# A float32 attend over four column quadrants, with scores and exponentials one head further ahead, and a part of a gate product in the last heads

## What is computed

```python
attn = _attention(rmsnorm(x, ln1_w), Wq, Wk, Wv, Wo)   # 16 heads of 32, causal, 512 x 512 probabilities
mod = 0.1 * tanh(attn @ A)                             # A: 512 x 16
h = rmsnorm(x, ln2_w)
gate = silu(h @ W_in.T + mod * (h @ A) @ B)            # 2048 wide
up = h @ W_up.T
out = x + gate * up @ W_down.T
```

## Time and profile before

| | |
|---|---|
| median of 3 runs | 1033.87 us |
| profiled execution | 1034.01 us |
| span from its first to its last instruction | 1032.3 us |
| TensorE busy | 1006.2 us (97%) |
| VectorE busy | 703.2 us (68%) |
| ScalarE busy | 604.1 us (59%) |
| GpSimd busy | 279.5 us (27%) |
| granted TensorE clock, mean | 0.998 |

### The profile page before, as it was taken

How to read it: one execution, slowest core, us unless ns; L and a number is a source line. 1 busy time by engine, 2 the same in 40 slices (tenths; PEclk the granted TensorE clock), 3 DMA queues, 4 the chain that set the end, 5 groups by cost and what they waited for, 6 DMA issues and landing times.

```text
span 1032.3 us, 16767 instructions
## 1 busy us (share of the span) xinstructions
PE 1006.2 (97%) x5140; PEld 831.6 (81%) x5141; DVE 703.2 (68%) x1841; ACT 604.1 (59%) x1447; POOL 279.5 (27%) x276
## 2 busy tenths in 40 slices
PE   6999999999999999999999999999999999999998
PEld 6787888877888888778888888778888887888886
DVE  7766756996665559985664489966655599754443
ACT  4464456996434448985344379963444499843332
POOL 4537124861000117640000148600001187300000
PEclk9999999999999999999999999999999999999999
DMA  6545124344232426434232354343334254222321
GB/s 233 194 161 173 41 100 117 82 93 163 92 91 91 132 60 183 95 111 147 91 92 91 113 159 93 77 166 96 94 100 145 58 157 101 84 82 91 91 91 52
DMA packets 47073, 115.78 MB, mean 112 GB/s; under 512 B 6800, under 2 KB 6800, under 8 KB 46096
## 3 DMA queue, kind: packets, MB, share of 16 engines
q1 hardware_dynamic: 43968, 105.06, 34.0%
q0 software_dynamic: 3040, 9.96, 2.8%
HBM read 76.46 MB, written 13.37 MB: 87 GB/s over the span
## 4 chain that ended last, share of the span: by engine, by line
PE 86%; POOL 6%; DVE 5%; DMA 1%; issue 1%; ACT 1%; SPq 0%; DVEq 0%
PE bank L537 67%; PE bank L800 6%; PE bank L737 6%; POOL big L493 3%; PE bank L703 2%; PE bank L842 1%; DVE big L1409 1%; PE bank L854 1%; POOL wqs L432 1%; PE bank L593 1%; DMA big<-in_x,gidx 1%; PE bank L608 1%; PE bank L771 1%; PE bank L651 1%; DVE wr L1440 1%
## 5 line engine op out<-in xcount | busy, mean ns | idle before, releaser
L537 PE MATMUL bank<-hT,wr 128*128 128x512 f32 x1488 | 358.1, 390 | 0.0
L537 PEld LDWEIGHTS bank<-hT,wr 128*128 128x128 f32 x1488 | 279.2, 188 | 60.6 <-issue 1.4
L537 PE MATMUL bank<-wr,actr 128*128 128x512 f32 (+1 forms) x1224 | 303.4, 397 | 0.8 <-issue 0.4
L537 PEld LDWEIGHTS bank<-wr,actr 128*128 128x128 f32 x1224 | 229.1, 190 | 49.2 <-issue 1.3
L493 POOL TENSOR_SCALAR big<-big,rr 128x256 f32<-128x256 f32 (+1 forms) x124 | 149.5, 1214 | 75.6 <-DVE rr L1415 75.2
L432 POOL TENSOR_TENSOR wqs<-wstage,wqs 128x512 fp32r<-128x512 f32 x32 | 43.2, 1360 | 433.6 <-ACT wqs L957 432.3
L1440 DVE SCALAR_TENSOR_TENSOR wr<-stream,lns,wr 128x256 fp32r<-128x256 f32 x256 | 121.7, 537 | 52.2 <-ACT wr L1069 52.2
L1042 ACT ACTIVATE big<-big,nb 128x512 f32<-128x512 f32 (+3 forms) x256 | 140.6, 560 | 9.3 <-DVE nb L1409 9.3
L1395 DVE TENSOR_TENSOR wr<-bank,wr 128x512 fp32r<-128x512 f32 (+1 forms) x224 | 125.7, 607 | 15.7 <-ACT wr L957 15.0
L957 ACT ACTIVATE wr<-bank 128x512 fp32r<-128x512 f32 (+1 forms) x224 | 110.6, 530 | 30.1 <-PE bank L537 17.8
L957 ACT ACTIVATE actr<-act_sb 128x512 fp32r<-128x512 f32 x64 | 40.4, 632 | 146.0 <-DVE act_sb L1454 146.0
(11 more groups left out here) (174 smaller groups left out, 991.1 us busy)
## 6 DMA issues: line engine op xcount, KB each, us to landing
stream<-in_wmlp SPq DMA_DIRECT2D x64, 512.0 KB, 4.1
stack<-wr SPq DMA_DIRECT2D x192, 128.0 KB, 2.3
stream<-in_wmlp SPq DMA_DIRECT2D x64, 256.0 KB, 2.7
big<-in_x SPq DMA_DIRECT2D x4, 1024.0 KB, 7.8
big<-y_rows SPq DMA_DIRECT2D x4, 1024.0 KB, 5.6
residual<-big SPq DMA_DIRECT2D x4, 1024.0 KB, 5.1
big<-residual SPq DMA_DIRECT2D x4, 1024.0 KB, 6.5
out<-big SPq DMA_DIRECT2D x3, 1024.0 KB, 4.8
```

The costliest lines, as they stand in the source:

```text
L537: mm = pe.matmul(dst, lhs(pl, k), rhs(pr, k), start=start and i == 0, stop=stop and i == n - 1, skip_group_check=skip)
```

## The change

Attend: the values are used as float32 as they are, and the turned probabilities are copied as float32, by ScalarE (banks 6 and 4) and VectorE (bank 5), with no low parts; they stand in two sets. The attend of a head is six products of 32 stationary columns (the head's 16 and those of the next, which land in rows that the next step of the sum does not use) written to four quarters of the 128 output partitions, 320 columns in each; the first four heads use one whole tile for each quarter instead. At the end of the batch the bank is copied, and one product with a 128 x 16 matrix of ones adds the quarters. The scaling of the 128-wide rows goes to GpSimd in heads 6 to 14. Scores are made four heads ahead in one go, maxima three ahead, exponentials, reciprocal and scaling two ahead. Projections are filled in one head earlier (heads 0 to 5, and two before the first step), the up quarters in heads 8 to 11, ahead of the attend. Eight of the twelve products of the first gate product are made in heads 13 and 14. The load of y waits for the last attend. GpSimd makes one of two copies of the modulation. The low rank copy and sum stand ahead of ScalarE's and VectorE's copies of head 15.

```diff
+ACT_HEADS = (0, 1, 2, 3, 4, 5, H - 1)
+def pool_tiles(head):
+    return (1,) if head == H - 1 else (1, 2) if head in ACT_HEADS else (1, 2, 0)
+PIECES = ((0, 320, 512, 1), (2, 256, 512, 3), (0, 0, 320, 0), (1, 128, 448, 2), (3, 384, 512, 1), (1, 448, 512, 3))
+COPY_AT = {(0, 0): (2, 0), (0, 2): (2, 1), (1, 0): (3, 0), (1, 2): (3, 1)}
...
-                sp.wait_ge(p_turned, b * (H * 3))
+                sp.wait_ge(pv_done, b * H)
                 sp.dma_start(hb, rows).then_inc(y_in, 16)
...
+                pool.wait_ge(z_ok, b + 1)
+                pool.wait_ge(zst_zero, 1)
+                g.tensor_copy(zst[64:64 + R, :], zrow).then_inc(zs_copy, 1)
...
+                def attend(kt, begin, end, quadrant):
+                    bk, col, _ = TURNED[kt]
+                    wide = R * min(2, H - head)
+                    return pe.matmul(bank[ATT][32 * quadrant:32 * quadrant + wide, begin:end],
+                                     vp_rows[:, kt, R * head:R * head + wide],
+                                     turned[j % 2][bk][:, col + begin - kt * P:col + end - kt * P],
+                                     start=head == 0, stop=False, skip_group_check=True)
...
+                    pe.wait_ge(pt_act, n * 2 + 2)
+                    pe.wait_ge(pt_dve, n + 1)
...
+                if head < H - AHEAD:
+                    scores(n + AHEAD, j % 2, stack_loads(b, head + AHEAD))
+                if UP_FROM <= head < UP_FROM + UP_PARTS:
+                    filling(b, head)
+                attend_all()
                 if head < H - 1:
                     wait_probs(n + 1)
                     for kt in TURN_ORDER:
                         turn_tiles(n + 1, other, kt)
...
+                if not UP_FROM <= head < UP_FROM + UP_PARTS:
                     filling(b, head)
...
                 pe.wait_ge(nb_ok, (b + 1) * H * 4)
-                gate_product(0)
+                pe.wait_ge(at_low, b + 1)
+                pe.wait_ge(rows_made, 1)
+                pe.matmul(bank[SUM][0:R, :], gather_rows[:, :], ysb[:, :], start=True, stop=True).then_inc(at_sum, 1)
+                gate_part(0, 8, DT * len(PARTS))
...
@@ ScalarE, head step @@
+                if head < H - 2:
+                    exponentials(n + 2, head + 2)
                 if (q, j) in COPY_AT:
                     split_qk(b, *COPY_AT[q, j])
...
+                act.wait_ge(p_turned, n * 3 + 1)
+                copy(turned[j % 2][6], bank[6][:, 0:256]).then_inc(pt_act, 1)
+                if head + 2 in ACT_HEADS:
+                    normalise(n + 2, head + 2)
+                act.wait_ge(p_turned, n * 3 + 3)
+                copy(turned[j % 2][4], bank[4][:, :]).then_inc(pt_act, 1)
...
@@ ScalarE, end of the batch @@
-                copy(att_low, bank[ATT][32:32 + R, :]).then_inc(at_low, 1)
+                copy(ysb[:, :], bank[ATT][:, :]).then_inc(at_low, 1)
...
@@ VectorE, head step @@
+                if head < H - 3:
+                    maxima(n + 3, (j + 1) % 2)
+                if head < H - 2:
+                    normalise(n + 2, j % 2)
+                if head == H - 1:
+                    dve.wait_ge(ha_low, b + 1)
+                    v.tensor_tensor(haT, bank[LOW_RANK][0:R, :], att_low, ALU.add).then_inc(ha_ok, 1)
                 if (q, j) in COPY_AT:
                     qk_low(b, *COPY_AT[q, j])
-                if two_more:
-                    maxima(n + 2, j % 2)
-                for i, (bk, w, at) in enumerate(TURNED_BANKS):
-                    dve.wait_ge(pt_hi, n * 3 + i + 1)
-                    low(pts[:, j % 2, LO, at:at + w], bank[bk][:, 0:w], pts[:, j % 2, HI, at:at + w], pt_lo)
+                dve.wait_ge(p_turned, n * 3 + 2)
+                v.tensor_copy(turned[j % 2][5], bank[5][:, :]).then_inc(pt_dve, 1)
...
@@ VectorE, ahead of head step 0 @@
+                maxima(b * H + 2, 0)
+                normalise(b * H + 1, 1)
```

More of the change, by code:

```diff
@@ L742, in turn_tiles @@
             def turn_tiles(n, par, kt, first=False):
-                if not first and kt != 3:
-                    pe.wait_ge(pt_lo, (n - 1) * 3 + PART_OF[kt])
+                if not first and kt == 1:
+                    pe.wait_ge(pt_dve, n)
+                elif not first and kt != 3:
+                    pe.wait_ge(pt_act, n * 2 - (kt == 2))
                 for qt in range(kt, TT):
@@ L777, in filling @@
             def filling(b, head):
-                project_part(b, head + 1)
+                if head < QH * 2 - 2:
+                    project_part(b, head + 2)
                 if head == UP_FROM:
@@ L795, in head_step, with attend_all @@
                 head, other = q * QH + j, (j + 1) % 2
[L797 to L802, removed]
+                def attend(kt, begin, end, quadrant):
[5 more added lines that the diff above has]
+                                     start=head == 0, stop=False, skip_group_check=True)
+                def attend_all():
+                    if head == 0:
+                        pe.wait_ge(vpa_ok, b + 1)
+                        pe.wait_ge(vpb_ok, b + 1)
+                    pe.wait_ge(pt_act, n * 2 + 2)
+                    pe.wait_ge(pt_dve, n + 1)
+                    if head < QUADRANTS:
+                        for kt in range(TT):
+                            mm = attend(kt, kt * P, S, (kt + head) % QUADRANTS)
+                    else:
+                        for piece in PIECES:
+                            mm = attend(*piece)
+                    mm.then_inc(pv_done, 1)
+                if head < H - AHEAD:
[3 more added lines that the diff above has]
+                attend_all()
                 if head < H - 1:
@@ L807, in head_step @@
                         turn_tiles(n + 1, other, kt)
[L808 to L826, removed]
-                    filling(b, head)
[L828 to L834, removed]
+                if not UP_FROM <= head < UP_FROM + UP_PARTS:
+                    filling(b, head)
             def gate_product(par):
@@ L838, in gate_product, with gate_part @@
                               lambda p, k: hT[:, p, k, :], DT, stop=False)
+            def gate_part(par, begin, end):
+                for i in range(begin, end):
+                    k, (pl, pr) = i // len(PARTS), PARTS[i % len(PARTS)]
+                    pe.matmul(bank[GATE[par]][:, :], wch[:, par, pl, k * P:k * P + P], hT[:, pr, k, :],
+                              start=i == 0, stop=False)
             def modulate(par):
@@ L910, in batch @@
                 turn_tiles(b * H, 0, 0, first=True)
[L911 to L912 removed]
+                scores(b * H + 3, 1, stack_loads(b, 3))
+                project_part(b, 1)
                 for q in range(NQ):
@@ L1115, in batch @@
                 split_qk(b, 1, 1, SECOND_K)
+                exponentials(b * H + 1, 1)
+                normalise(b * H + 1, 1)
                 for q in range(NQ):
                     for j in range(QH):
+                        if q == NQ - 1 and j == QH - 1:
+                            act.wait_ge(ha_done, b + 1)
+                            act.wait_ge(y_stored, 16 * ITEMS)
+                            copy(att_low, bank[LOW_RANK][32:32 + R, :]).then_inc(ha_low, 1)
                         head_step(b, q, j)
```

108 lines of the change are left out of this document (45 added, 63 removed).

## The result

The changed kernel takes 1140.17 us (median of 4 runs, 1135.19 to 1142.82) beside 1033.86 for the kernel before: ratio 1.1022, 95% interval 1.0984 to 1.1061, so 10% slower. The forecast was slower, 1108 us with a range of 1070 to 1145. The profiled execution is the quickest of the four, 1135.19 us with a span of 1133.4; the span grew by 101.1 us.

A forecast was written before the change was run, and what follows sets the result against it. The prediction had TensorE and VectorE work pacing the kernel before, and a closed loop over three probability buffers after; 18.5 us more in each of four batches, 74 us on 1034.01, gave 1108 us, range 1070 to 1145.

The forecast's parts named there:

- What bounds the kernel now: Head steps before the change: TensorE paces heads 1 to 6 at 4.26 us, VectorE's work the others at 3.78.
- the closed loop: Head steps: with three probability buffers, maxima of head n+3 wait for turns of head n; links sum to 4.36 + x.
- x: Time of one head's float32 attend on TensorE: 0.28 to 1.14 us if quarters run side by side, 0.70 taken.
- Rival 2: Attend: the quarters do not overlap, x is 1.14 to 4.6 us; at 2.2, +90 us, 1198 us; chance 0.10.
- the wide attends: Heads 0 to 3, whole tiles: longest part 512 columns instead of 320, 0.42 us more each, +1.7 a batch.
- The sum of the steps: Heads 0 to 12 of a batch: thirteen steps of 5.06 us, 65.8, plus extras, 72.0 against 53.8 before.
- Step 0: First head step of a batch: late exponentials of head 2 add a wait of 0.7 us.
- the granted clock: Sign of being wrong: a clock below 0.99 in the stage, which idle time might bring; not priced.
- The load of y: Load moved to the last attend, about 3.3 us later against the gate stage; costed at nothing, bound 1 us a batch.
- The start: Start of a batch's head steps: half a projection now stands ahead of the first turns, +1.4 us.
- Rival 1: Head steps: the loop does not bind, the longest work sets steps of 3.8 or 3.7 us; 1019 us; chance 0.12.
- Rival 3: Attend to turns: TensorE drains on each change of tiles, 0.17 us a head, +11 us, 1119 us; chance 0.15.

The follow-up runs named there:

- one-quarter kernel: Changed kernel with all attend products written to the first 32 output partitions instead of four quarters: 1227.23 us.
- filled kernels: Changed kernel with three extra 512-column score products per step in TensorE's waits: 1138.84 us in 48 steps, 1135.43 us with the first step of each batch left out.
- the scores behind the turns: Changed kernel with turned copies first on VectorE and ScalarE, and scores of head n+4 made after the turns of head n+1: 1054.07 us.
- open order: Changed kernel with turned copies first, scores after the next head's turns, and ScalarE's high part of q or k after its copies: 1033.12 us.

## Why the prediction was right, and where it was short

- **What bounds the kernel now** and **the closed loop** held. The sum of the links, 4.36 + x, was 5.06; the clean step is 5.11. With the low part of q or k it is 5.71, the 0.60 more that was summed.
- **x** was taken at 0.70, the middle of two far ends; it is 0.67 to 0.68, with a pause of 0.10 in it that the term did not have. That was luck within wide ends. Rival 2 (no overlap) is excluded by the one-quarter kernel: serial is 2.25. Of the wide attends 0.42 was added, 0.28 is measured (steps of 5.39 and 5.98).
- **The sum of the steps.** For steps 1 to 11 the terms give 58.7 us a batch; where no slow stretch falls they take 58.9. Step 0 was summed as 6.8 and took 6.5 to 7.3, partly for another reason: the stack, not the exponentials, was last. "Together 72.0 against 53.8" was right but for the clock.
- **The step that failed**, inside a total that held, is the last one of the text, which names it as a sign of being wrong: the granted clock "which the idle time might bring and which I have not priced". Steps 1 to 11 took 246.2 us where the filled kernels' batches with full clock give 4 x 58.9 = 235.5: 10.7 us. Step 12, where TensorE idles for 3.1 us, has 1.8 more than summed, and most of the 5 us at the end of the batches stands beside half-clock turns in head 13. In all some 17 of the 27.1 us between 74.0 forecast and 101.1 measured. Turns or attends at half clock stand in every one of these places; that idle time brings them is argued from them and from the filled kernels. The other three runs' clocks (0.968 to 0.972 beside 0.974) go with their 4 to 8 us more.
- **The load of y** "I cost at nothing, with 1 us a batch as its other bound": it was 1.8 to 1.9 us in three batches, 5.6 in all, above my bound. I had compared when all loads were in and not when the first weights were wanted. The loads of the stack, behind the residual in the same queue, I had not followed at all.
- **The start** was +1.5, +1.5 and +2.2 us in three batches (forecast 1.4), and 3.4 in the first, where 2 us fall in the expert stage. They go with the clock there: from 36 to 42 us it was 0.50 in the changed kernel's trace, whose turns start at 181.2 us, and 1.00 with the scores behind the turns, which has the same code there and starts at 177.9 (0.72 in the kernel before, 177.7).
- **Rival 1** (the loop does not bind) is what the open order made true: its steps, 3.8 with a projection, are 3.91. GpSimd's three tiles were put at 3.7 us and take 3.02, so the other steps came out at 3.2 to 3.7. The forecast for it was 1019. The open order alone gave 1033; 1021.6 was reached by another order, with the loads and the end of the batch moved too, so that the two numbers are close is luck.
- **Rival 3** (a drain for each change of tiles) is not excluded, and the trace speaks for a part of it. That the sum closes to 0.05 says nothing, as x was free and was measured up to the turns. With whole tiles, an attend, then the weight loads of the turns in a later step:

```profile
433.24 0.62 PE L804 MATMUL bank<-act_sb,big 128*32 128x512 f32 x1
...
433.69 0.59 PE L804 MATMUL bank<-act_sb,big 128*32 128x512 f32 x1
434.22 1.31 PE L734 MATMUL bank<-ident,big 128*128 128x128 f32 x10
```

```profile
489.90 0.53 PEld L804 LDWEIGHTS bank<-sil,big 128*32 128x32 f32 x5
490.53 1.07 PEld L734 LDWEIGHTS bank<-ident,big 128*128 128x128 f32 x10
```

  The two instructions of a 512-column product start 0.45 us apart, the turns 0.53 behind the second. With six products the last instruction, of 64 columns, starts 0.16 us ahead of the turns, where two such instructions of the one-quarter kernel follow each other at 0.06. So some 0.10 us a head, of the 0.17 forecast, lies inside x, about 6 us in all; the weight loads of the turns do not run ahead there. Between the 48-column attends and the 128-column products of the kernel before there is no such pause: 512 columns take 0.23 us to the next start whatever comes next. No run takes the change of tiles away, so whether it is the cause stays open.

## What to carry to other kernels

When work is moved one step further ahead, count the buffers it needs: with as many buffers as steps ahead, the producer waits for this step's consumer, and everything queued behind it on its engine joins a loop whose length is a sum of latencies, whatever work was saved. Look for such a loop by following one wait through each engine's order until it returns, and open it by order first: what the next consumer wants (copies, loads) goes ahead of what is made for later. Price the idle time that a loop leaves on TensorE as well, since slow stretches came with it here.

## What the hardware showed that I had not expected

- Two-instruction float32 products overlap over four quarters of the output partitions: 12 instructions in 0.68 us against 2.25 in one quarter, each with about 0.10 us of pause ahead of the 128-column turns behind it. The eight wide instructions of the first heads take 0.95 to 0.98 for a longest part of 512 columns.
- The granted clock fell to 0.50 for 3 to 10 us at a time in the changed kernel, behind steps in which TensorE had sat idle for 0.9 to 3.1 us at a time. The one-quarter kernel, whose attends of 2.25 us leave the same waits in the steps, has such stretches too (0.50 from 496 to 498 us, behind a wait of 1.5; mean 0.986). One cost 0.8 to 3.0 us in the steps. The mean clock differs from run to run (0.968 to 0.974), and the changed kernel's runs spread by 7.6 us where those of the kernel before spread by 0.7 beside them and by 2.1 later.
- GpSimd's scaling of three tiles takes 3.02 us where two take 2.45: a 128-wide tile costs 0.60, half of a 256-wide one (1.21), while a 384-wide one costs the same (1.24).
